# Edge stage: the one-hot comparisons written as scalar comparisons with an accumulator

## The reference, cut to what matters

```
msg_in = concatenate([x[src], x[dst], edge_attr])            # per edge
msgs   = maximum(msg_in @ mW1 + mb1, 0) @ mW2 + mb2
agg    = segment_sum(msgs, dst) / clip(count, 1)
upd    = maximum(concatenate([x, agg]) @ uW1 + ub1, 0) @ uW2 + ub2
out    = layernorm(upd + x) * gamma + beta
```

## Time and profile before

| | us |
|---|---|
| median of three runs | 4737.0 (4735.77 to 4737.39) |
| the profiled execution, its own time | 4734.76 |
| span of its instructions | 4732.5 |
| edge stage: first gather begins, last gather begins | 1376.4, 3579.8 |

### The profile page before, as it was taken

One profiled execution on the slowest core, in us unless ns is written; L12 is line 12 of the kernel. 1 busy time (PEld: TensorE's weight loads), 2 busy tenths in 40 slices (PEclk: granted clock), 3 DMA queues, 4 the chain that ended last, 5 costly groups with the idle time before them and its releaser, 6 DMA issues.

```text
span 4732.5 us, 100585 instructions
## 1 busy us (share of the span) xinstructions
PE 4136.1 (87%) x35231; PEld 3736.8 (79%) x35231; DVE 2962.8 (63%) x8183; ACT 1925.0 (41%) x4164; POOL 1977.7 (42%) x2199
## 2 busy tenths in 40 slices
PE   1499999999987788888888888888888999999997
PEld 1499999999975678778787787787888777777876
DVE  6799999999953344444444444444445667777777
ACT  1555666566631222222222222212213666666664
POOL 5611111111127777777777777777772000000000
PEclk9799999999998899999999999999999999999999
DMA  5444444444455566676776666766768787887885
GB/s 120 163 204 207 207 209 208 208 204 204 204 187 138 146 202 206 199 209 202 205 209 203 203 207 198 212 198 199 208 205 253 229 240 209 248 237 214 264 250 164
DMA packets 793921, 967.67 MB, mean 204 GB/s; under 512 B 124439, under 2 KB 674055, under 8 KB 781143
## 3 DMA queue, kind: packets, MB, share of 16 engines
q1 hardware_dynamic: 623488, 764.12, 48.0%
q0 software_dynamic: 60048, 125.37, 10.5%
q10 hardware_dynamic: 110151, 75.61, 6.1%
HBM read 707.25 MB, written 257.60 MB: 204 GB/s over the span
## 4 chain that ended last, share of the span: by engine, by line
POOL 34%; PE 20%; issue 12%; DVE 2%; DMA 2%; ACT 1%; ACTq 0%; POOLq 0%; DVEq 0%
POOL ACC L1047 34%; PE ps L1957 8%; PE ps L1958 8%; DMA ACC<-table,ACC 1%; PE ps L1873 1%; PE ps L1993 1%; PE ps L1975 1%; PE ps L1962 1%; DVE COUNTS L2560 1%; ACT COUNTS L1381 0%; PE ps L1984 0%; PE ps L1824 0%; DVE H L2763 0%; DVE ST L2715 0%; DVE BIG L2487 0%
## 5 line engine op out<-in xcount | busy, mean ns | idle before, releaser
L1047 POOL DMA_INDIRECT ACC<-table,ACC x1715 | 1682.1, 981 | 615.2 <-issue 516.7
L1858 PE MATMUL ps<-BIG 128*128 128x257 f32 x3430 | 862.4, 394 | 146.9 <-ACT BIG L1248 146.5
L2487 DVE TENSOR_TENSOR BIG<-ps,ACC 128x512 f32<-128x512 f32 (+1 forms) x441 | 297.8, 675 | 1088.4 <-DMA ACC<-table,ACC 905.3
L1858 PEld LDWEIGHTS ps<-BIG 128*128 128x128 f32 x3430 | 634.2, 195 | 249.7 <-ACT BIG L1248 170.4
L1248 ACT ACTIVATE BIG<-BIG 128x512 f32<-128x512 f32 (+1 forms) x441 | 273.7, 621 | 1325.5 <-DVE BIG L2487 1322.5
L1581 PE MATMUL ps<-H,ACC 128*128 128x128 f32 x4802 | 689.9, 284 | 0.0
L1381 ACT ACTIVATE COUNTS<-X 128x512 fp32r<-128x512 bf16 (+1 forms) x1092 | 600.9, 599 | 161.0 <-PE ps L1958 154.8
L1581 PEld LDWEIGHTS ps<-H,ACC 128*128 128x128 f32 x4802 | 588.0, 191 | 0.2 <-ACT ACC L1189 0.2
L1189 ACT ACTIVATE BIG<-ps 128x392 bf16<-128x392 f32 x784 | 390.3, 498 | 468.2 <-PE ps L1567 468.2
L1957 PE MATMUL ps<-COUNTS,H_BIG 128*128 128x512 f32 (+1 forms) x1274 | 509.5, 400 | 30.8 <-ACT COUNTS L1381 15.0
L1958 PE MATMUL ps<-COUNTS,H_BIG 128*128 128x512 f32 (+1 forms) x1274 | 489.0, 384 | 0.0
(11 more groups left out here) (292 smaller groups left out, 7566.7 us busy)
## 6 DMA issues: line engine op xcount, KB each, us to landing
X<-count_mat SPq DMA_DIRECT2D x360, 512.0 KB, 4.8
weight_mat<-ACC SPq DMA_DIRECT2D x49, 3136.0 KB, 9.2
BIG<-in_edge_attr SPq DMA_DIRECT2D x392, 256.0 KB
count_mat<-BIG SPq DMA_DIRECT2D x49, 1568.0 KB, 12.8
REL_WT<-weight_mat SPq DMA_DIRECT2D x275, 256.0 KB
BIG<-rel_tab ACTq DMA_DIRECT2D x392, 128.0 KB
BIG<-weight_mat SPq DMA_DIRECT2D x176, 256.0 KB
X<-count_mat SPq DMA_DIRECT2D x108, 384.0 KB, 3.7
```

The costliest lines, as they stand in the source:

```text
L1047: pool.indirect_dma_start(GR[:, q * QUAD + u, :], None, tables[1], bass.IndirectOffsetOnAxis(ap=STEP_IDX[:, b % 3, r * QUAD + u:r * QUAD + ...
L1858: mm = pe.matmul(PS[4 + par][:, 0:HIW], DR[:, q * QUAD + u, :], HB[:, q * QUAD + u, :], start=(r == 0 and u == 0), stop=(r == QB - 1 and u ...
L2487: dve.tensor_tensor(HB[:, steps, 0:F], PS[n % 2][:, 0:size * F].rearrange("p (u f) -> p u f", f=F), GR[:, own, :], ALU.add).then_inc(rows_ ...
```

## The change

Both comparisons become `tensor_scalar` with a second operation, an addition, and an `accum_out`: the sum of each row of the comparison is also written, to a small array `HITS` that nothing reads. The transposed one-hot stays one instruction per quad. The one-hot of the steps, one `tensor_tensor` per quad before, becomes one `tensor_scalar` per step, with the column of `REL` as scalar of its partition; the last of a quad signals.

```diff
+        HITS = of_acc(at + 11 * F, EQ * (QUAD + 1))[0].rearrange("p (q u) -> p q u", u=QUAD + 1)
...
             def dense_turned(n):
...
-                dve.tensor_scalar(DTB[:, q, cols], RELB[:, q, cols], svec[:, 0:1], None, ALU.is_equal).then_inc(dt_ready, 1)
+                dve.tensor_scalar(DTB[:, q, cols], RELB[:, q, cols], svec[:, 0:1], None, ALU.is_equal, ALU.add,
+                                  accum_out=HITS[:, q, QUAD:QUAD + 1]).then_inc(dt_ready, 1)
...
             def dense_onehots(n):
...
-                dve.tensor_tensor(DR[:, q * QUAD:q * QUAD + size, :],
-                                  iota[:, :].rearrange("p (a d) -> p a d", a=1).broadcast_to([P, size, P]),
-                                  REL[:, step:step + size].rearrange("p (u a) -> p u a", a=1).broadcast_to([P, size, P]), ALU.is_equal).then_inc(onehot_ready, 1)
+                for u in range(size):
+                    last = dve.tensor_scalar(DR[:, q * QUAD + u, :], iota[:, :], REL[:, step + u:step + u + 1], None, ALU.is_equal, ALU.add,
+                                             accum_out=HITS[:, q, u:u + 1])
+                last.then_inc(onehot_ready, 1)
```

## The result

The changed kernel takes 4693.63 us (median of four runs, 4690.94 to 4695.36), the kernel before 4736.39 on the same chips: a ratio of 0.9911, 95% interval 0.9900 to 0.9923, 42.8 us less. 4696 was forecast. The profiled execution took 4695.36 us with a span of 4693.6.

What follows compares the result with a forecast made beforehand. POOL's gathers were taken to bound the kernel, with a tail from DVE comparisons holding them. 41.2 us from the gathers less 0.2 at the ends gives 41; 4737.0 - 41 = 4696 us, range 4690 to 4714.

Steps and rivals of the forecast that it cites:

- The cause: Gathers beginning under a DVE comparison already started need something 0.126 us after their start and get it when it ends.
- line 2494's 39.6 us: Wide tensor_tensor with two SBUF inputs: 159 gathers begin under it, held 39.6 of the tail's 42.6 us; all would go.
- line 2478's 1.6: Bf16 comparison of the transposed one-hot: held a further 20 gathers for 1.6 us, expected to go too.
- The accumulator form holds nothing: New comparisons on DVE hold no gather, from fifteen DMAs of 0.95 or 0.96 us under line 2077; 41.2 us together.
- the rival that bf16 holds: Accumulator comparison in bf16, line 2478, still holds gathers for its longer length: tail 50 us, time 4745; chance 0.04.
- What DVE pays: Longer comparisons on DVE: 0.89 us more per quad, some 390 us over 441 quads, inside its idle time.
- The covers: Two checks that DVE's added time stays beside other work: POOL's buffers and PE not becoming the slower one.
- POOL's buffers: Gathers reusing a buffer after line 2487's addition: tightest case 18.4 us later, so under a microsecond of delay can't reach POOL.
- PE's later one-hots: PE's first products of a quad wait for line 2478: 0.52 us lost at the sixth quad, at most 1.4 per block.
- PE's reserve: PE's idle time per block: 5.9 us before, 5.1 us left once a block is 0.84 us shorter.
- PE taking part back: Late one-hots at two or three quads of a block delay PE; half the gain lost, 4716 us; chance 0.07.
- DVE and PE as the bound: Each quad's 0.89 us comes whole onto PE, 7.7 us a block, POOL's buffers fill: 4805 us; chance 0.05.

Runs made afterwards that it cites:

- the extra accumulator comparison: Changed kernel plus one 512-column accumulator-form comparison per quad into DR, overwritten afterwards by the usual ones: 4690.24 us, 0.9906 of before.
- the last experiment: Changed kernel with one gather fewer in each quad from the thirteenth on, an earlier quad's rows added instead: 4349.96 us, ratio 0.9184.

## Why the prediction was right

**The cause** is as it was put: gathers that begin under line 2494 waited for its end. Put back alone, the instruction brings the tail back (45.9 and 43.3 us); taken away alone, it takes nearly all of it away (6.6 us left). No semaphore stands behind this wait, though the engines were said to wait for each other through semaphores only: the program has none between line 2494 and a gather, and the profile shows the wait not as idle time but as a longer gather.

**The size.** Forecast 41.2 us from the gathers and 41 in all; 42.2 went from the tail, 42.8 from the median. The term that was small is line 2494's 39.6 us in 159 gathers: with the exact starts and ends of the trace, of which the views show two decimals, 164 gathers held 40.7 us, and with line 2478's 1.6 that is more than 42. The short block instructions with two SBUF inputs kept theirs, as forecast: 1.4 us before and 1.3 after, in some 20 gathers. The tail shows only 0.4 because the gathers that nothing holds average 0.9555 us and not 0.956.

**The accumulator form holds nothing**, which was read off the preparation's fifteen gathers under line 2077 for float32. A sixteenth, the first of that chain, began at 10.58 under the same line and took 1.15 us; it came after 8.45 us of idle time, it was not held until the end of its comparison, which would have been 0.56 us more, and what made it longer is not shown. For bf16 no row existed; now 205 gathers under line 2479 show it, and the rival that bf16 holds (4745 us) falls. The rule of the Trainium skill, page "SBUF — State Buffer", section "Who interferes with whom", which leaves the accumulator form out of those that take the shared ports, agrees with the trace: 0.966 us at most for both types.

**What DVE pays**: 0.89 us a quad were worked out and some 390 us over the stage; the pitches are 0.67 and 0.27 as taken from the earlier trace rows, but DVE's busy time rose by 355 us, 0.80 a quad. That is why 689.5 us of idle time are left ahead of the addition and not some 650. This term was a little too large, and nothing hung on it.

**The covers.** POOL's buffers: the tightest case is 15.7 us now, against 18.4. PE's later one-hots, in the waits of its weight loads over the stage, first before, then after:

```profile
PEld ps L1846 <- DVE BIG L2478: 12.0, 16, 2.8
PEld ps L1847 <- DVE BIG L2479: 24.0, 40, 3.1
```

At the sixth quad 0.52 us a block were to be lost; about 10 of the 24.0 us lie there, in 32 cases, 0.3 each, where it was one case before. Most of the rest is at the third quad, as it was before. So less was lost than worked out. That the wait on line 1793 takes such delays up, as the prediction said, is shown by the extra accumulator comparison, where it became shorter by more than PE's wait for line 2479 grew. What was wrong here is the size of PE's reserve: it was counted as 5.1 us a block at the clock of that stage, and the last experiment shows 44.2 - 37.5 = 6.7.

**The rivals.** PE taking part back, and DVE and PE as the bound, both fall with the extra accumulator comparison: one more instruction of 0.73 us on DVE per quad on top of the change, and no more time.

What isn't shown is what exactly the gather needs at 0.126 us. That the rule goes by SBUF inputs, and not by tensor_tensor as such, rests on instructions the kernel has (line 2489 with one input in PSUM: 173 gathers begin under one that ends more than 0.126 us after their start, 0.955 us on average); the same comparison with an input in PSUM was not run.

## What to carry to other kernels

Where a chain of gathers binds, look at the distribution of one gather's duration, not at its mean: a median on the floor with a tail beside it asks what was running when the long ones began, and the excess over the floor is what can be won. A DVE instruction off the critical path can be made slower with profit, if its form no longer holds the engine that is on it; that pays as long as its own waits have room. Short instructions hold for less time than one long one of the same work, so even without the form most of the loss can be cut away.

## What the runs showed that was not expected

A plain comparison cut into 128 columns is nearly as good as the accumulator form (tail 5.0 against 0.4 us) and loads DVE less: four of them have a pitch of 0.78 to 0.80 us, four with accumulator 1.07. And PE's busy time was no fixed amount of work: the same products needed 38.7 us a block (1489.04 us over 1700 / 44.2 blocks) while PE stood idle for 5.5 us a block and the granted clock was 0.94, and 36.7 (1271.56 over 1300 / 37.5) when it hardly waited and the clock stayed at 1.00. The wait between a gather and a comparison goes both ways: with the plain form, a comparison that begins about halfway through a gather ends only when the gather is over, and that time is DVE's.
